# Sixteen unread products per batch on TensorE in the edge loop of a two-layer graph network

## The reference, cut to what matters

```python
for h in range(8):
    feat = x @ W[h]
    logit = leaky_relu((feat @ a1)[src] + (feat @ a2)[dst], 0.2)
    m = segment_max(logit, src)
    e = exp(logit - m[src])
    att = e / segment_sum(e, src)[src]
    agg = segment_sum(att[:, None] * feat[dst], src)
    outs.append(relu(agg))
```

## Time and profile before

| | |
|---|---|
| time of 3 runs | 3004.78, 3007.24, 3007.37 us; median 3007.24 |
| span of the profiled execution | 3541.0 us |
| TensorE, VectorE busy in it | 76%, 61% |
| GpSimd, ScalarE busy in it | 52%, 28% |
| mean granted TensorE clock | 0.883 of 2.4 GHz |

### The profile page before, as it was taken

One profiled execution on the slowest core, in us unless ns is written; L12 is line 12 of the kernel. 1 busy time (PEld: TensorE's weight loads), 2 busy tenths in 40 slices (PEclk: granted clock), 3 DMA queues, 4 the chain that ended last, 5 costly groups with the idle time before them and its releaser, 6 DMA issues. The chain is left out here.

```text
span 3541.0 us, 46052 instructions
## 1 busy us (share of the span) xinstructions
PE 2699.5 (76%) x10647; PEld 1671.1 (47%) x10692; DVE 2161.8 (61%) x3783; ACT 995.2 (28%) x3078; POOL 1858.0 (52%) x1883
## 2 busy tenths in 40 slices
PE   6887377777777877777777787877778788788991
PEld 4554256666656656655656652323333333233440
DVE  9999966666666767666668743333333333334668
ACT  6733334444443444434444520000000000000220
POOL 0000255555555556555555446666666666664667
PEclk8998678898988899898898897888889999999995
DMA  5110366666666666666665856666666666565226
GB/s 184 47 40 31 111 180 185 186 189 185 180 182 188 180 191 189 183 192 176 177 189 191 288 152 174 176 180 178 178 176 178 173 173 175 171 174 157 67 66 251
DMA packets 243449, 588.25 MB, mean 166 GB/s; under 512 B 57744, under 2 KB 82832, under 8 KB 243400
## 3 DMA queue, kind: packets, MB, share of 16 engines
q0 software_dynamic: 133120, 443.52, 43.8%
q1 hardware_dynamic: 110280, 144.14, 12.4%
HBM read 533.43 MB, written 54.10 MB: 166 GB/s over the span
## 5 line engine op out<-in xcount | busy, mean ns | idle before, releaser
L506 POOL DMA_INDIRECT big<-feat_table,idx x880 | 841.3, 956 | 1020.8 <-ACT idx L531 407.5
L1133 POOL DMA_INDIRECT big<-h_table,idx x784 | 743.6, 948 | 460.6 <-issue 235.2
L801 PE MATMUL psA<-big,onehot 128*128 128x260 f32 x1760 | 504.0, 436 | 120.1 <-DVE big L683 95.4
L801 PE MATMUL psB<-big,onehot 128*128 128x260 f32 x1760 | 479.8, 420 | 18.6 <-DVE acc L693 13.1
L801 PEld LDWEIGHTS psA<-big,onehot 128*128 128x128 f32 x1760 | 365.4, 216 | 208.3 <-issue 115.2
L557 ACT ACTIVATE big<-big,late_weights 128x65 f32<-128x65 f32 x1760 | 434.4, 343 | 0.0
L801 PEld LDWEIGHTS psB<-big,onehot 128*128 128x128 f32 x1760 | 351.5, 209 | 84.9 <-DVE acc L693 22.2
L531 ACT CAST idx<-minorB 128x8 int32 (+1 forms) x101 | 20.4, 204 | 1142.6 <-DMA big<-h_table,idx 1142.6
L1565 DVE TENSOR_TENSOR acc<-acc,psCD 128x512 f32 x176 | 120.7, 686 | 320.1 <-remote 106.2
L1565 DVE TENSOR_TENSOR acc<-acc,psA 128x512 f32 x176 | 120.7, 686 | 273.6 <-remote 103.3
L1859 PE MATMUL psA<-big,onehot 128*128 x352 | 199.3, 650 | 58.9 <-issue 42.7
(11 more groups left out here) (447 smaller groups left out, 3960.8 us busy)
## 6 DMA issues: line engine op xcount, KB each, us to landing
nodes_all<-slot_nodes SPq DMA_DIRECT2D x56, 512.0 KB
big<-feat_table,idx POOLq DMA_INDIRECT x880
feat_table<-big SPq DMA_DIRECT2D x49, 264.0 KB, 2.1
x_table<-acc SPq DMA_DIRECT2D x49, 256.0 KB, 3.8
h_table<-big SPq DMA_DIRECT2D x49, 256.0 KB, 4.0
big<-h_table,idx POOLq DMA_INDIRECT x784
big<-h_table SPq DMA_DIRECT2D x49, 256.0 KB, 2.6
big<-x_table SPq DMA_DIRECT2D x49, 256.0 KB, 4.3
```

The source lines that it names most:

```text
L506: g.indirect_dma_start(ring[:, b.k, q * SB + u, :], None, feat_table, bass.IndirectOffsetOnAxis(ap=idx[:, 2 * b.k + q, u:u + 1], axis=0)). ...
L801: ins = pet.matmul(psum[:, 512 * hf:512 * hf + HALF_W], onehot[:, q, u % SB, :], ring[:, b.k, u, HALF_W * hf:HALF_W * (hf + 1)], start=(u ...
L1133: g.indirect_dma_start(big[:, place:place + D], None, h1_table, bass.IndirectOffsetOnAxis(ap=idx[:, r.c % CHUNK_CYCLE, b:b + 1], axis=0)). ...
```

## The change

A helper `keep_busy` issues products of the 128x128 float32 identity with itself into 128 columns of the bank of `this` batch that nothing else uses (columns 256 to 383). No engine reads them, they wait for nothing and they signal nothing. In a pass with both `this` and `nxt`, of which there are 54, six of them stand between lot 5 and `spread_carries`, and ten stand at the end of step 7, behind lot 7 of `this` batch, and so ahead of lot 0 of the next one.

```diff
+        idle_ps = [ps[:, 256:256 + P] for ps in (psD, psE)]
...
+            def keep_busy(b, products):
+                for n in range(products):
+                    pet.matmul(idle_ps[b.k], ident, ident, start=True, stop=True)
+
             def pass_batch(this, nxt):
...
                     if a == 5:
+                        if this:
+                            keep_busy(this, 6)
                         spread_carries(nxt)
+                    if a == LB - 1 and this:
+                        keep_busy(this, 10)
                     if a == 6:
```

## The result

The changed kernel took 3092.61 us (median of three runs, 3090.78 to 3094.79) against 3007.24. The ratio on record is 1.0293, with a 95% interval of 1.0278 to 1.0307; the plain quotient of the two medians is 1.0284. That is 85 us more, where 133 more were forecast. It lies in the forecast's own range.

The account below looks back on a forecast made before the run. It took a TensorE-VectorE round trip in layer 0's loop as the bound: 1.4 + 2.0 - 0.5 - 0.4 = 2.5 us a batch, times 54 = 135, on 3007 gives 3142 us (rounded 3140); own range 3060 to 3190, 8-in-10 range 2965 to 3200.

Parts of the forecast that it names:

- The stray waits: VectorE's waits of unknown origin in layer 0's loop: only in the profiled execution, 277 us of the loop's 1447.
- the six rows: Profile rows of VectorE's waits of unknown origin: 274 us in layer 0, 255 us in layer 1's loop, together 529.
- The price of a product: On TensorE, two passes of 0.115 us each; all sixteen products 3.7 us a batch at 2.4 GHz.
- Six products exposed: Ahead of `spread_carries`: all of their time delays the batch, 1.4 us.
- Ten exposed: Ahead of lot 0: 2.3 us less a gap of about 0.3 us, so 2.0 us a batch exposed.
- What is given back: Per batch: 0.5 us from TensorE's vanishing waits for `acc`, 0.4 us from a higher clock.
- No engine is full.: Layer 0's loop, 1447 us: TensorE fullest at 1127 us (78%), VectorE 987, GpSimd 816, so a round trip bounds it.
- The rival that I gave 0.07: No change: GpSimd's gathers set the pace, the products lie in TensorE's slack; 3007 us, chance 0.07.
- The round trip that the prediction took for the limit: Layer 0's loop: TensorE sends VectorE a small product, VectorE scans and returns it, and in-order TensorE stands still when that is late.
- The clock's rival: Gaps are real, products fill them and hold TensorE at 2.4 GHz: gain at most 116 us, about 2950; chance 0.23.
- Places: Idle of L779 (58.9 us) and lot 0's wait for L683 (95.4 us) go near zero; L788's idle stays.
- The signs in the profile: Expected: passes 0.11 to 0.12 us apart, full-clock batches 24 us or more. Against: clock 0.97 or more with shorter stage.

Follow-up runs that it names:

- the new profile of before: The kernel before, unchanged, profiled once more: span 3002.5 us, plain run 3004.29 us.
- the load on GpSimd: Four unread memsets a batch on GpSimd from the third batch on: kernel before 3025.4 us against 3002.5; changed kernel 3093.79 us, ratio 1.0305.

## Why the prediction was right, and which term was mis-sized

The direction, the price of the products and their exposure were right, and so was the range. What bounds the kernel before was not, and there the number owes something to luck. Taken as they stand, the prediction's terms would give 22 us for seven products behind lot 7 (14 x 0.115 - 0.3 - 0.9 = 0.41 a batch), 26 for the six alone and 59 for the ten alone. Measured are 2, 41 and 20: seven and ten are far off, and the order of six and ten is the wrong way round.

The starts in the two batches above give the balance, changed kernel against before:

| stretch of TensorE's batch | before, us | after, us | difference |
|---|---|---|---|
| lot 5 to `spread_carries` (six products) | 1.90 | 3.24 | +1.34 |
| lot 7 to lot 0 (ten products) | 2.25 | 4.08 | +1.83 |
| lot 0 to the last product of `turn_logits` | 9.65 | 7.69 | -1.96 |
| from there to `sum_ends` | 2.18 | 2.49 | +0.31 |
| the batch | 20.17 | 21.69 | +1.52 |

54 x 1.52 = 82 of the 85 us.

- **The stray waits.** Right. They were of that one execution. The loop of the new profile of before is some 335 us shorter than in the old one, more than the 277 that I took off: 20.2 us a batch and not 21.3. Layer 1's loop is some 195 us shorter (its additions at L1565 run from 1753.6 to 2720.6 us, and in the old profile from 2097.4 to 3259.1), where my split left 257. That the six rows came to 529 us, so near the 533.8, was chance: they are VectorE's waits alone, and in layer 0's loop ScalarE had 224 us of such waits and GpSimd 111 besides. In the new profile the clock does not fall either, so the 0.8 us a batch that I left for the clock was not there.
- **The price of a product.** Right: 0.115 us a pass was taken. `L810` needs 2.39 us for twenty and 1.50 for twelve, so 0.89/8 = 0.111. The doubled products, at 193 to 198 us, agree with the rows' 200. The Trainium skill's 81 ns ("TensorE: Matmul & The Clock Gate", "Back-to-back issue gap"), which gave an estimate of 140 us at most, is too low for these float32 passes, which are 111 ns apart.
- **Six products exposed.** 1.4 predicted, 1.34 measured. **Ten exposed:** 2.0 predicted, 1.83 measured.
- **What is given back.** This is the term of the sum that was mis-sized. I took 0.5 us for waits for `acc` and 0.4 for the clock, 0.9 together. Measured is 1.96 - 0.31 = 1.65, and 1.46 of the 1.96 is one wait that I did not count, for gathered rows ahead of `turn_logits`. The rest of the 1.96 are smaller ones, such as that of lot 1 to lot 2. Putting 1.65 in place of 0.9 turns 2.5 us a batch into 1.75; the other 0.23 is what the two exposures were smaller than taken.
- **"No engine is full."** This reading was wrong and led to the missed wait. GpSimd was busy for 816 of 1447 us in the old profile, and for 814 of 1110 in the new one, 73%, where TensorE had 91% and VectorE 89%. Yet it was the pace: the 0.30 us between two gathers are not counted as busy, and in 900 us no gather started less than 0.29 after the one before had ended. (A memset found room for 0.13 of its 0.22 us there, as the load on GpSimd shows.) The rival that I gave 0.07, gathers that set the pace with the products in TensorE's slack, had the right pace and not enough slack: it holds for seven products behind lot 7 (3004.85 us) and fails for sixteen, and for six ahead of `spread_carries`. The round trip that the prediction took for the limit is real, but has 0.4 to 0.7 us a batch to spare in the kernel before, by the estimates above.
- **The clock's rival.** It fell. The loop ran at 0.99 before and 1.00 after, so there was next to nothing to win: 0.01 x 1110 is 11 us. The rule of the Trainium skill that the prediction quoted ("TensorE: Matmul & The Clock Gate", "Part 1: The HAM clock gate"), that activity releases the throttle, is not contradicted: the undisturbed loop had TensorE busy for 91% and a clock of 0.99 without the products.
- **Places.** I expected the idle ahead of L779 and lot 0 to go to zero (it did, but in the undisturbed kernel before there was none and 0.24 us to fill), and L788's idle to stay. The 2.33 us there were a stray wait as well, as reckoned: in the new batch of before L788 has no bracket.
- **The signs in the profile.** Batches of 24 us or more were expected and took 21.69, because the profile of the changed kernel had no stray waits at all; the forecast had reckoned with them in it. So its span did shrink, but not because such waits hid the products. The clock of 1.00 and the shorter loop, named as a sign against the forecast, came true in the profile and not in the plain runs.

What stays open: the 5 us of the bfloat16 products (0.1 us a batch) are clear of zero by their interval, and nothing in their profile was found for them. What caused the stray waits was not looked for; no other profile of this case had them. Nor was the round trip of TensorE and VectorE tested by an experiment of its own: it is read from one profile.

## What to carry to other kernels

Work on an engine that has slack is free up to the slack and costs its whole time from there on, and the slack is that of the place as well as that of the engine. Seven products, 1.56 us, behind lot 7 were free, and so were six at the wait for rows; the same six, 1.34 us, cost 41 us where VectorE was waiting for what stood behind them. Of sixteen, 3.6 us, 1.5 us a batch were paid; of the next sixteen all 3.6. Look for the pace in the pitch of an engine's starts, not in its busy share: sixteen starts some 1.25 us apart were the batch, at a busy share of 73%, the lowest but one of the four engines. And when a profile's span is not that of the plain runs, ask which waits have no known origin, and take the profile again before reading clocks or gaps from it.

## What had not been expected of the hardware

One profiled execution was 18% longer than the plain runs (3541.0 against 3007), and twelve others, of the same and of close kernels, were not: each was within 0.3% of its kernel's plain median. The extra time lay in the two loops that gather, some 335 and 195 us of it; the first 440 us, the sort, took the same in both. These loops are where the waits without a known releaser stand, on VectorE up to 4.8 us long in layer 0's. Only two more, of 8.8 and 4.2 us, lie outside, both ending at 448.5 us. Along with them came a granted clock of 0.89 instead of 0.99 in layer 0's loop, where TensorE was busy for 78% and not 91%. That the idle time is what made the clock fall was not tested. A reader of that profile alone finds two gaps and a slow clock, and products that seem to fill the one and cure the other.
